# Narrower node ranges in the build, the next head's scaled features one block earlier, denominators by a product, and complement counts for some source tiles of a four-layer graph kernel

## The reference, cut to what matters

```
x = (meta_x @ W).reshape(N, HEADS, DIM)
a_src = sum(x * att_src, -1);  a_dst = sum(x * att_dst, -1)
logits = leaky_relu(a_src[src] + a_dst[dst], 0.2)
ex = exp(logits - seg_max[dst])
alpha = ex / (segment_sum(ex, dst)[dst] + 1e-16)
out = segment_sum(x[src] * alpha, dst).mean over heads + bias
```

## Time and profile before

| | |
|---|---|
| median of 3 executions | 1333.14 us (1330.76 to 1335.65) |
| profiled execution, its own time | 1330.93 us |
| its span, first to last instruction | 1329.1 us |
| PE, DVE, ACT, POOL busy | 88%, 67%, 48%, 5% of the span |
| mean granted TensorE clock | 0.917 |

### The profile page before, as it was taken

How to read it: one execution, slowest core, us unless ns; L and a number is a source line. 1 busy time by engine, 2 the same in 40 slices (tenths; PEclk the granted TensorE clock), 3 DMA queues, 4 the chain that set the end, 5 groups by cost and what they waited for, 6 DMA issues and landing times.

```text
span 1329.1 us, 40769 instructions
## 1 busy us (share of the span) xinstructions
PE 1172.1 (88%) x16951; PEld 1104.9 (83%) x16951; DVE 885.7 (67%) x2402; ACT 635.2 (48%) x1251; POOL 63.0 (5%) x113
## 2 busy tenths in 40 slices
PE   0588778878999999999998799599989989998996
PEld 0577778778999999999976699489979978997996
DVE  1899999996444344444723624787777777777787
ACT  0676676662000000000112102677878788787886
POOL 2000000001111111110000102000000000000000
PEclk9876777678999999999998799599999999999999
DMA  1544444430000000000000000000000000000000
GB/s 27 81 65 63 65 61 66 62 58 10 3 3 2 3 2 3 2 3 3 3 1 2 2 2 2 2 1 2 2 1 2 2 2 1 2 1 2 7 11 12
DMA packets 133692, 21.47 MB, mean 16 GB/s; under 512 B 132961, under 2 KB 133378, under 8 KB 133538
## 3 DMA queue, kind: packets, MB, share of 16 engines
q1 hardware_dynamic: 132190, 18.75, 9.4%
q10 hardware_dynamic: 1252, 0.31, 0.1%
q0 software_dynamic: 96, 0.16, 0.1%
HBM read 18.41 MB, written 0.80 MB: 14 GB/s over the span
## 4 chain that ended last, share of the span: by engine, by line
PE 63%; DVE 25%; issue 5%; ACT 5%; DMA 1%; SPq 0%; POOL 0%; DVEq 0%; ACTq 0%; POOLq 0%
PE bank L1629 33%; PE bank L1754 16%; PE bank L1750 9%; DVE ohk L924 7%; DVE ohp L926 4%; DVE raw L914 2%; ACT Mr L835 2%; DVE Mr L1405 2%; ACT F L798 1%; DVE F L1314 1%; DVE eaT L1306 1%; PE bank L1540 1%; PE bank L1745 1%; DVE xs L1167 1%; DVE ohj L884 1%
## 5 line engine op out<-in xcount | busy, mean ns | idle before, releaser
L1629 PEld LDWEIGHTS bank<-GH,C 128*128 128x128 f16 x8025 | 451.5, 98 | 8.3 <-issue 5.1
L1629 PE MATMUL bank<-GH,C 128*128 128x128 f16 x8025 | 453.6, 220 | 4.4 <-DVE GH L979 4.4
L1754 PE MATMUL bank<-F,Mr 128*128 128x260 f16 (+1 forms) x2538 | 364.5, 274 | 10.8 <-DVE Mr L1405 7.8
L835 ACT ACTIVATE Mr<-eaT,steep 128x640 f16<-128x640 f32 x433 | 325.7, 821 | 36.4 <-PE bank L1754 35.7
L1405 DVE TENSOR_TENSOR Mr<-Mr,C 128x640 f16<-128x640 f16 x433 | 199.4, 488 | 99.1 <-ACT Mr L835 97.7
L1754 PEld LDWEIGHTS bank<-F,Mr 128*128 128x128 f16 x2538 | 225.4, 98 | 34.8 <-DVE Mr L1405 6.8
L1750 PE MATMUL bank<-FN,C 128*128 128x130 f16 x2500 | 232.7, 221 | 0.6 <-DVE r L1323 0.6
L706 ACT ACTIVATE plo<-bank 128x256 f32<-128x256 f32 (+1 forms) x91 | 32.9, 361 | 400.1 <-PE bank L1629 389.8
L1084 DVE TENSOR_TENSOR S<-bank,plo 128x256 f32<-128x256 f32 (+1 forms) x91 | 36.0, 395 | 246.2 <-ACT plo L706 246.2
L1750 PEld LDWEIGHTS bank<-FN,C 128*128 128x128 f16 x2500 | 186.2, 98 | 13.7 <-DVE r L1323 1.1
L1540 PE MATMUL bank<-ohk,ohp 128*128 128x100 f16 (+3 forms) x1210 | 159.5, 282 | 10.8 <-ACT C L666 7.4
(11 more groups left out here) (224 smaller groups left out, 841.3 us busy)
## 6 DMA issues: line engine op xcount, KB each, us to landing
raw<-in_edges_dram SPq DMA_DIRECT2D x242, 68.0 KB, 2.1
xs<-in_x_dram SPq DMA_DIRECT2D x1, 800.0 KB, 4.9
out_dram<-xs SPq DMA_DIRECT2D x4, 160.0 KB
wg<-in_L_gnn_W_dram ACTq DMA_DIRECT2D x2, 64.0 KB
z<-in_L_gnn_att_src_dram SPq DMA_DIRECT2D x1, 128.0 KB, 2.7
z<-in_L_gnn_att_dst_dram SPq DMA_DIRECT2D x1, 128.0 KB, 3.1
out_dram<-xs SPq DMA_DIRECT2D x1, 128.0 KB
wts<-in_L_gnn_W_dram ACTq DMA_DIRECT2D x3, 16.0 KB
```

The lines of the kernel that those rows point to most:

```text
L835: act.activation(Mr[:, mi % RB, :], nadS, ACT.Sigmoid, bias=steep[:, h, t:t + 1], scale=-STEEP / XS).then_inc(s_step, 1)
L1629: last = pe.matmul(bank[:, b, jj * 2 * D:(jj + 1) * 2 * D], C[:, t, (t0 + jj) * P:(t0 + jj + 1) * P], GH[:, par, t, :], start=t == 0 and j ...
L1754: return pe.matmul(bank[:, k, a_:z_], Mr[:, mi % RB, j * P:(j + 1) * P], F[:, t, a_:z_], start=start, stop=t == T - 1)
```

## The change

What it does:
- Build: slot 1's range goes from nodes 2-13 to 2-11, slot 2's from 5-13 to 6-13; six products a window instead of five; 650 instead of 725 columns. The attribute work (`high_attrs`, `low_attrs`, `rest`) is done in two halves of a group instead of four units.
- Denominators: a one-row product puts the constant XS into a 65th column beside `xw`'s result, so `scaled`, `high_f` and `low_f` carry it along; the arrays and copies for it go.
- Two buffers for the scaled features; parts 0 and 1 of the next head are multiplied and scaled in block 3, part 2 in block 4; `high_f` and `low_f` stay in block 4.
- Complement: for 16 units of each of the heads 0 to 2 (b = 1, 2 with t = 0, 4, ..., 20; b = 3 with t = 0, 7, 14, 21) DVE makes N = M - C in one buffer `Nr`, and PE does two products of 130 columns, `M @ F[first half]` and `N @ F[second half]`, in place of one of 260 and one of 130.

```
-    PART = ((0, 0, 6), (1, 2, 6), (1, 6, 13), (2, 5, 13), (3, 9, 13))
-    NODES = ((0, 6), (2, 13), (5, 13), (9, 13))
+    PART = ((0, 0, 6), (1, 2, 6), (1, 6, 11), (2, 6, 11), (2, 11, 13), (3, 9, 13))
+    NODES = ((0, 6), (2, 11), (6, 13), (9, 13))
...
+        def apart(h, b, t):
+            return h < H - 1 and (b in (1, 2) and t % 4 == 0 and t < T - 1 or b == 3 and t % 7 == 0)
...  ACT, build_group
-                    if w in (0, 3):
-                        low_attrs(i, par, 2 + w // 3)
-                    if more and w in (6, 9):
-                        low_attrs(i, par + 1, w // 3 - 2)
-                    if more and w + 1 in [u_[1] for u_ in UNITS]:
-                        high_attrs(i, par + 1, [u_[1] for u_ in UNITS].index(w + 1))
+                    if w == 0:
+                        low_attrs(i, par, 1)
+                    if more and w == 9:
+                        low_attrs(i, par + 1, 0)
+                    if more and w in (5, 10):
+                        high_attrs(i, par + 1, w // 10)
...  DVE, build_group
-                    if u < 2:
-                        rest(i, par, u + 2)
-                    elif more:
-                        rest(i, par + 1, u - 2)
+                    if u == 0:
+                        rest(i, par, 1)
+                    elif more and u == 3:
+                        rest(i, par + 1, 0)
...  ACT, high_f
-                    act.activation(pairs_of(t0)[:, :, 0, 0:D], Vx.rearrange("p t e d -> p (t e) d"), ACT.Copy, scale=1.0 / LO).then_inc(s_fhi, 1)
-                    act.activation(F[:, t0:t0 + NT, :].rearrange("p t (a c) -> p t a c", c=S1)[:, :, :, D],
-                                   den[:, :, :, h, t0:t0 + NT].rearrange("p e l t -> p t (e l)"), ACT.Copy).then_inc(s_fhi, 1)
+                    act.activation(pairs_of(t0)[:, :, 0, :], Vx[gi % 2].rearrange("p t e c -> p (t e) c"), ACT.Copy, scale=1.0 / LO).then_inc(s_fhi, 1)
...  DVE, scaled
-                    if gi:
-                        v.wait_ge(s_F, gi)
+                    if gi >= 2:
+                        v.wait_ge(s_F, gi - 1)
...  DVE
+                def complement(h, b, t):
+                    ni = APART[h, b, t]
+                    v.wait_ge(s_M, unit(h, b, t) + 1)
+                    if ni >= RN:
+                        v.wait_ge(s_Nu, ni - RN + 1)
+                    v.tensor_tensor(Nr[:, ni % RN], Mr[:, unit(h, b, t) % RB, :], C[:, t, b * NT * P:(b + 1) * NT * P], ALU.subtract).then_inc(s_N, 1)
...
+                            if b == NG - 2 and h < H - 1 and t in (10, 18):
+                                scaled(h + 1, (t - 10) // 8)
                             if b == NG - 1 and h < H - 1:
-                                if t in (8, 15, 22):
-                                    scaled(h + 1, (t - 8) // 7)
-                                elif t in (12, 17, 24):
+                                if t == 14:
+                                    scaled(h + 1, 2)
+                                elif t in (12, 17, 22):
                                     low_f(h + 1, (t - 12) // 5)
...
+                            if t and apart(h, b, t - 1):
+                                complement(h, b, t - 1)
...  PE, xw
+                    pe.matmul(pxw[:, :, D], own16, own16[:, 0:NT], start=True, stop=False)
...  PE, the loop over t
+                            dense_t = [t for t in range(ahead) if not apart(h, b, t)]
...
-                            else:
+                            elif not apart(h, b, t):
                                 for j in range(0 if t >= ahead else lead, NT):
                                     plain(BANKS[b][j], t0 + j, t, False)
...
+                                if apart(h, b, t):
+                                    last = masked(k, mi, j, t, 0, 2 * S1, t == 0 and j >= lead)
...
                             last.then_inc(s_Mu, 1)
+                            if t and apart(h, b, t - 1):
+                                ni = APART[h, b, t - 1]
+                                pe.wait_ge(s_N, ni + 1)
+                                for j in range(NT):
+                                    last = pe.matmul(bank[:, BANKS[b][j], 2 * S1:4 * S1], Nr[:, ni % RN, j * P:(j + 1) * P], F[:, t - 1, 2 * S1:4 * S1], start=False, stop=False)
+                                last.then_inc(s_Nu, 1)
```

More of the change, by code:

```diff
@@ L64, in gnn_kernel @@
     RB = 6
+    RN = 1
     NG = 5
@@ L308, in steps, with unit_of @@
             return sum(by_act(h_, b_, t_) for h_ in range(H) for b_ in range(NG) for t_ in range(T) if (h_, b_, t_) <= (h, b, t))
+        def apart(h, b, t):
+            return h < H - 1 and (b in (1, 2) and t % 4 == 0 and t < T - 1 or b == 3 and t % 7 == 0)
+        APART = {}
+        for h_ in range(H):
+            for b_ in range(NG):
+                for t_ in range(T):
+                    if apart(h_, b_, t_):
+                        APART[h_, b_, t_] = len(APART)
+        def unit_of(mi):
+            return mi // (NG * T), mi // T % NG, mi % T
         def pairs_of(t0):
@@ L681, in _ @@
             positions(0, 0)
-            for u in range(NU):
+            for u in range(2):
                 high_attrs(0, 0, u)
-            for u in range(2):
-                low_attrs(0, 0, u)
+            low_attrs(0, 0, 0)
             with act.Fori(0, G // 2 - 1) as i:
@@ L829, in _ @@
                                 high_f(h, 3 + t // 16)
-                            if b == NG - 1 and h < H - 1 and t in (11, 16, 23):
+                            if b == NG - 1 and h < H - 1 and t in (11, 16, 21):
                                 high_f(h + 1, (t - 11) // 5)
@@ L942, in _ @@
             c.here()
-            for u in range(2):
-                rest(0, 0, u)
+            rest(0, 0, 0)
             with v.Fori(0, G // 2 - 1) as i:
@@ L1735, in xw @@
                     pe.wait_ge(s_nads, blk + 1)
+                    pe.matmul(pxw[:, :, D], own16, own16[:, 0:NT], start=True, stop=False)
                     for j in range(NT):
                         for e in range(2):
-                            last = pe.matmul(pxw[:, j * D:(j + 1) * D], xT[:, (g * NT + j) * P:(g * NT + j + 1) * P], whl[:, e, h * D:(h + 1) * D], start=j == 0 and e == 0, stop=j == NT - 1 and e == 1)
+                            last = pe.matmul(pxw[:, j, 0:D], xT[:, (g * NT + j) * P:(g * NT + j + 1) * P], whl[:, e, h * D:(h + 1) * D], start=False, stop=j == NT - 1 and e == 1)
                     last.then_inc(s_xw, 1)
@@ L1770, in _ @@
                                 pe.wait_ge(s_ring, before(h, b, j))
-                            for t in range(ahead):
-                                plain(BANKS[b][j], t0 + j, t, t == 0)
+                            dense_t = [t for t in range(ahead) if not apart(h, b, t)]
+                            for t in dense_t:
+                                plain(BANKS[b][j], t0 + j, t, t == dense_t[0])
                         for t in range(T):
@@ L1795, in _ @@
                                 k = BANKS[b][j]
-                                if t == 0 and j < lead:
+                                if apart(h, b, t):
+                                    last = masked(k, mi, j, t, 0, 2 * S1, t == 0 and j >= lead)
+                                elif t == 0 and j < lead:
                                     masked(k, mi, j, t, 0, 2 * S1, False)
```

76 lines of the change are left out of this document (41 added, 35 removed).

## The result

The changed kernel takes **1314.82 us** (median of 4 executions, 1312.94 to 1315.06), beside 1331.96 for the kernel before on the same chip: ratio 0.9864, 95% interval 0.9841 to 0.9887. It is faster by 1.4%, 17.1 us where the forecast (1306) had some 26, so about two thirds of it. The profiled execution spans 1311.0 us, 18.1 less than before; its own time is 1312.94.

A forecast was written before the change was run, and what follows sets the result against it. DVE was taken to bound the build, PE the middle attention blocks, an ACT-DVE hand-over the head ends. Terms -12.3 - 6.4 - 8.0 + 0.5 = -26.2 us from 1330.93 gave 1304.7, median 1306.9, predicted 1306; range 1294 to 1319.

The forecast's parts named there:

- the likeliest case: Whole kernel: build gains in full, complement half given back, head ends mostly cured; 1299 to 1312 us, chance 0.50.
- the build doesn't follow: Build, rival: PE or ACT takes DVE's place as limit, -4 instead of -12.3 us, giving 1314; chance 0.11.
- Build: forecast -12.3: Build: shorter one-hots and two fewer subtractions on DVE, less waits for PE; -12.3 us, between -13.1 and -4.
- DVE's own sum: Build: DVE saves 0.424 us of one-hots and 0.17 of subtractions, 0.59 a group, 13.1 us over 22 groups.
- my walk: Build: ACT finishes the second half's `high_attrs` 0.2 to 0.4 us ahead of DVE's subtraction, so nothing was charged.
- alone does not turn the result: Build: at 1.2 GHz throughout, PE needs 10.2 us a group, still under DVE's 11.4.
- Complement: forecast -6.4: Attention layer: 48 units save 0.27 us each, -13.0, less 6.6 of new waits; -6.4 us, between -13 and 0.
- In front of `nad`: Wait (a): the path to M of unit 24 has no slack; 0.5 us charged in blocks 1 and 2, 0.35 in block 3.
- At t = 4: Wait (b): PE reaches unit 4 before its M is ready; 0.55 us charged in block 1, 0.3 in block 2, 0 in 3.
- the rival in which ACT and DVE take the layer over: Attention layer, rival: subtraction nearer 0.88 us or single N buffer keeps DVE behind PE; 1316 us, chance 0.20.
- Head ends: forecast -8.0: Blocks 3 and 4: ACT-DVE hand-over goes, 1.4 us of wait left instead of 3.87; -8.0 us, between -11.5 and -1.
- Denominators: forecast +0.5: Attention layer: twenty ACT copies go, twenty one-row products come at nothing to 0.06 us each; +0.5 us, between -1 and +1.2.

The follow-up runs named there:

- three pieces: Changed kernel with the attribute work in three pieces (windows 0 to 5, 6 to 8, 9 and 10) instead of two halves: 1305.34 us.
- The table of four builds: Group times by node ranges and attribute work: wide with units 12.01 us, narrow with units 11.55, wide with halves 12.03, narrow with halves 11.86.
- the fillers: Changed kernel with ten added 128-column products a group, results unused, in PE's idle time: 1311.42 us.
- the units back: Changed kernel with the attribute work back in the four units of before, narrow ranges kept: 1307.54 us.
- the full product: Changed kernel with the constant column beside `xw` made by a product of 128 rows instead of one row: 1312.01 us.
- Undoing the move: Changed kernel with all `xw` and `scaled` of the next head back in block 4, two buffers and constant column kept: 1323.41 us.
- the three units ahead of `nad`: Changed kernel with unit 20 of blocks 1 and 2 and unit 21 of block 3 no longer apart: 1311.67 us.
- the units elsewhere: Changed kernel with units apart at t = 2, 6, ..., 22 in blocks 1 and 2 and 1, 8, 15, 22 in block 3: 1317.68 us.

## Why the prediction was right or wrong

The sign and the range held, and so did the attention layer but for the denominators; the likeliest case and the order of the parts did not: the build was to give most and gave least. What came was the rival "the build doesn't follow", priced at 1314 with a chance of 0.11. That 1314.8 lies in the range is owed to its upper end, which was drawn to take that rival in.

**Build: forecast -12.3, measured -2.5** (by the first `nad`; the last `ohp` of the build starts 3.6 earlier, at 298.58 instead of 302.17, and the longer stretch behind the hops takes 1.3 back). DVE's own sum was right: with nothing late the same instructions make 11.39 us a group in the change's own trace, where 12.01 less 0.59 had been forecast, and three pieces brought 11.7 us. The step that failed is the one on ACT, "by my walk through the queues it is done 0.2 to 0.4 us ahead, so I take nothing". It is late by some 0.4 in 20 groups of 22, and even with windows at the high level it is through only just in time (256.01 for a subtraction at 256.07). Two things made my walk too short. The two halves stand behind each other on ACT around the last eviction, 0.74 and 0.75 us. And I kept PE at the mix of clock levels of before; it fell to the low one in nearly every group, which brings the last windows later. The sentence that the clock "alone does not turn the result" looked at whether PE becomes the bound; it does not, but it releases ACT, and ACT releases DVE. The table of four builds shows that the halves do no harm alone and hurt with the narrow ranges, and the fillers show that the clock has a share. The Trainium skill's rule that I set beside this rival ("TensorE: Matmul & The Clock Gate", "The HAM clock gate": activity releases the throttle) points the way the trace went: fewer columns, clock 0.50 instead of 0.71. But with the units back the same fewer columns ran at 0.64, so the columns alone don't make the whole fall; whether the wait itself holds the clock down was not tested.

**Complement: forecast -6.4, measured -7.1** (2.35 a head; 5.8 by the medians). By its steps: the unit's 0.27 is right (narrow products 56 to 58 ns). In front of `nad` I charged 0.5, 0.5 and 0.35; measured are 0.52, 0.52 and 0.46. At t = 4 I charged 0.55, 0.3 and 0; measured 0.26, 0.29 and 0. The subtraction ran in the fast form, 488 ns, so the rival in which ACT and DVE take the layer over fell.

**Head ends: forecast -8.0, measured -8.3.** Block 4 went from 26.74 to 23.71 (forecast 23.4), with 1.33 us of wait left (forecast 1.4). With the full product it is 23.52; block 3 grew by 0.64 (22.22 less 21.59, less 0.38 for two one-row products, plus the 0.39 that the complement took from it; forecast 0.65), and block 0 lost 0.19, where nothing had been forecast: -3.22 + 0.64 - 0.19 = -2.77 a head. Undoing the move cost 5.9 without the clock's part, 1.95 a head; the rest of the 2.77 is that block 0 and, for 0.57, the one-row products, which cost PE nothing while it waits in block 4.

**Denominators: forecast +0.5, between -1 and +1.2; measured about +1.5** (0.57 in each of three heads by the run with the full product, less 0.26 by which the first head's block 0 got shorter); 2.8 us by the medians came back with the full product. The step that failed priced a one-row product at 0.06 us at most, "a pair as above"; it costs 0.2 us.

Together the attention layer was forecast at -13.9 and came at -14.1 without the slow block of before's profile. That it fits so closely is in part luck: the denominators cost 1.0 more than forecast, and the other two parts gave 1.0 more. The miss of the whole, 9 us, is the build's 9.8.

## What to carry to other kernels

When instructions are merged to save their fixed cost, look at who waits for the larger piece: the engine that bounds a stage goes at its own pace only while what it needs comes back from the others in time, and the size of the pieces is part of that way. Walk such a path at the low clock level of TensorE too, above all if the change takes work from it; an engine needn't become the bound to be late. And where a wait with no slack stands behind a stretch, what is saved in front of it is worth nothing: the three units ahead of `nad` gave nothing.

## What was not expected of the hardware

A one-row product in a stream of 128-row ones costs 0.2 us (from the N products' end at 925.00 to 925.20, where the next products start), while the same column by a 128-row product costs 0.03 (923.51 to 923.54). The two also take their operands from different tiles, which was not separated. With halves in both, taking a tenth of the columns from the build's products (725 to 650 a window) went with a fall of the granted clock of the stretch from 0.71 to 0.50, and PE got busier by it (41.63 of 48 us instead of 39.09). With units in both it went from 0.71 to 0.64.

The record of the granted clock can be wrong. With the units elsewhere the build is that of the change, instruction for instruction, and its group takes 11.84 us as against 11.86, but its row says full clock:

```profile
132.00:180.00 48.00, 41.61 (x630) 40.95 (x628) 46.29 (x123) 32.31 (x75) 0.00 (x0) 1.00 0.44 64
```

PE's windows in it stand 0.89 us apart, as at the low level in the change's trace, and not 0.64; up to 192 us the rows of this run show full clock throughout. Nor do the means of whole executions follow the time: the four of the changed kernel have 0.884, 0.933, 0.879 and 0.879 at 1312.9 to 1315.1 us. The distance of like instructions is the surer sign. Taken by how long the `ohk` products of a window last, 93 of 100 windows of the build are at the low level in the change, 61 before and 68 with the fillers, which bears out the rows used above.
